# A channel mix by one 96x96 block for each time half, with 20 unread identity products ahead of its loop

## The reference

```python
att = jnp.einsum('bnd,bmd->bnm', left, xf) / jnp.sqrt(jnp.float32(dk))
att = jax.nn.softmax(att, axis=-1)
return (att @ xf).reshape(sh) if requires_value else att
...
xc = jnp.swapaxes(_attention(jnp.swapaxes(x, 1, 2), W1_c, W2_c, True), 1, 2)
xt = jnp.swapaxes(_attention(jnp.swapaxes(xc, 1, 3), W1_t, W2_t, True), 1, 3)
```

## Time and profile before

| | us |
|---|---|
| median of three runs | 1740.32 |
| the three runs | 1743.68, 1740.32, 1725.60 |
| the profiled execution | 1733.57 |
| its span, first to last instruction | 1731.7 |
| TensorE busy in the span | 1425.5 (82%), mean granted clock 0.90 |
| VectorE, ScalarE, GpSimd busy | 1051.8, 768.2, 609.1 |

### The profile page before, as it was taken

How to read it: one execution, slowest core, us unless ns; L and a number is a source line. 1 busy time by engine, 2 the same in 40 slices (tenths; PEclk the granted TensorE clock), 3 DMA queues, 4 the chain that set the end, 5 groups by cost and what they waited for, 6 DMA issues and landing times. The chain is left out here.

```text
span 1731.7 us, 27002 instructions
## 1 busy us (share of the span) xinstructions
PE 1425.5 (82%) x8422; PEld 1185.3 (68%) x8422; DVE 1051.8 (61%) x2259; ACT 768.2 (44%) x1222; POOL 609.1 (35%) x910
## 2 busy tenths in 40 slices
PE   6698999997582599999999956788999996377676
PEld 5596887886582488888888846687888885244443
DVE  5323788887348445444445326463788887488885
ACT  5322555554350233233333225223555554288885
POOL 1100456556212445566555321000455656100000
PEclk9799999999675699999999965798999999599999
DMA  7451121211581255565555278821121221112322
GB/s 237 123 157 38 47 73 64 78 58 64 192 265 57 69 115 112 131 140 99 112 124 109 31 161 288 261 83 37 47 82 55 81 68 60 55 56 84 100 88 64
DMA packets 97738, 180.13 MB, mean 104 GB/s; under 512 B 15184, under 2 KB 33152, under 8 KB 97668
## 3 DMA queue, kind: packets, MB, share of 16 engines
q1 hardware_dynamic: 75396, 135.16, 24.8%
q0 software_dynamic: 16384, 31.51, 10.6%
q10 hardware_dynamic: 5888, 12.59, 2.0%
HBM read 113.12 MB, written 66.10 MB: 103 GB/s over the span
## 5 line engine op out<-in xcount | busy, mean ns | idle before, releaser
L922 PE MATMUL g_y<-L_z,L_pt 128*128 128x192 f32 x1024 | 195.4, 334 | 1.5 <-ACT L_pt L1137 0.5
L922 PEld LDWEIGHTS g_y<-L_z,L_pt 128*128 128x128 f32 x1024 | 165.2, 192 | 6.8 <-ACT L_pt L1137 6.8
L1082 POOL TENSOR_TENSOR L_xr<-L_xr,L_lnb 128x192 f32<-128x192 f32 x128 | 105.5, 852 | 177.8 <-DMA L_xr<-x 92.0
L1455 POOL DMA_INDIRECT sums<-x_yo,x_places x64 | 102.9, 1609 | 141.9 <-ACT x_yo L1658 131.9
L1129 ACT ACTIVATE L_e<-g_s,L_nm 128x512 f32<-128x512 f32 x128 | 88.0, 687 | 78.8 <-DVE L_nm L970 77.5
L890 PE MATMUL g_z<-L_kw,L_xnT 96*128 96x192 f32 x512 | 91.8, 331 | 20.6 <-DVE L_v L1000 20.4
L1089 POOL TENSOR_TENSOR L_t<-L_rstd 128x48 f32<-128x48 f32 x96 | 28.9, 301 | 223.7 <-DVE L_rstd L1024 218.7
L1567 DVE TENSOR_TENSOR x_mid<-ex_g,x_sig 128x480 f32<-128x480 f32 (+1 forms) x48 | 31.4, 654 | 123.4 <-ACT x_sig L1649 123.4
L890 PEld LDWEIGHTS g_z<-L_kw,L_xnT 96*128 96x128 f32 x512 | 82.3, 189 | 29.9 <-DVE L_v L1000 29.9
L979 DVE SCALAR_TENSOR_TENSOR L_p<-L_e,L_rl,L_adj 128x512 f32<-128x512 f32 x128 | 99.1, 775 | 4.5
L970 DVE TENSOR_REDUCE L_nm<-g_s 128x1 f32<-128x512 f32 x128 | 87.5, 683 | 18.8 <-PE g_s L899 18.0
(11 more groups left out here) (345 smaller groups left out, 3890.6 us busy)
## 6 DMA issues: line engine op xcount, KB each, us to landing
L_xnT<-xn_rows SPq DMA_DIRECT2D x48, 384.0 KB, 3.3
x<-L_y SPq DMA_DIRECT2D x32, 384.0 KB, 2.6
xn_rows<-L_xnT SPq DMA_DIRECT2D x54, 192.0 KB, 3.9
L_xr<-in_x SPq DMA_DIRECT2D x24, 384.0 KB, 3.4
L_xr<-x SPq DMA_DIRECT2D x24, 384.0 KB, 3.4
L_raw<-xn_rows SPq DMA_DIRECT2D x16, 384.0 KB, 3.6
ff_xa<-x SPq DMA_DIRECT2D x16, 384.0 KB, 3.9
ff_xr<-x SPq DMA_DIRECT2D x16, 384.0 KB, 3.5
```

Source lines behind the costliest of these rows:

```text
L922: last = nc.tensor.matmul(out, pt[k % 2][:, P * c:P * c + P], z[q][:, c, :], start=False, stop=(c == NK - 1))
L1082: last = nc.gpsimd.tensor_tensor(v_, v_, gain(s.lnb), ALU.add)
L1455: nc.gpsimd.indirect_dma_start(sums, row(places[e % 2][:, 1, t:t + 1]), yo[t % 4][:, :], None, compute_op=ALU.add).then_inc(sent[t % 4], 16)
```

## The change

A time half's outputs depend on the same half's inputs alone. The changed kernel makes one 96 x 96 matrix for each item (16 channels x 6 time steps, the same for both halves) instead of two of 96 x 192. Each product then gives the 96 outputs of its own half and nothing is added up in PSUM; to keep the order of the outputs, channel by channel with 12 time steps each, a product writes 16 runs of 6 elements, 12 apart. The number of products is unchanged. Ahead of TensorE's loop stand 20 products of the 128 x 128 identity with itself into the first PSUM buffer, which the first item overwrites.

```diff
                 def big_matrix(b):
                     if b >= 2:
                         dve.wait_ge(mixed, ready(b - 2))
-                    for h in range(2):
-                        last = nc.vector.tensor_tensor(
-                            big[b % 2][0:HALF, h, :].rearrange("p (c t) -> p c t", t=T),
-                            s.rct[0:HALF, b * C:b * C + C].unsqueeze(2).to_broadcast([HALF, C, T]),
-                            s.tmask[:, h, 1, :].unsqueeze(1).to_broadcast([HALF, C, T]), ALU.mult)
-                    last.then_inc(big_done, 1)
+                    nc.vector.tensor_tensor(
+                        big[b % 2][0:HALF, 0, 0:HALF].rearrange("p (c t) -> p c t", t=TH),
+                        s.rct[0:HALF, b * C:b * C + C].unsqueeze(2).to_broadcast([HALF, C, TH]),
+                        s.tmask[:, 0, 1, 0:TH].unsqueeze(1).to_broadcast([HALF, C, TH]), ALU.mult).then_inc(big_done, 1)
...
                     for k in range(NK):
+                        cols = psm[z % 2][:, k // 2, CT * (k % 2):CT * (k % 2) + CT].rearrange("p (c t) -> p c t", t=T)
                         for h in range(2):
-                            last = nc.tensor.matmul(psm[z % 2][:, k // 2, CT * (k % 2):CT * (k % 2) + CT],
-                                                    xnT[z][0:HALF, h, P * k:P * k + P], big[z % 2][0:HALF, h, :],
-                                                    start=(h == 0), stop=(h == 1))
+                            last = nc.tensor.matmul(cols[:, :, TH * h:TH * h + TH],
+                                                    xnT[z][0:HALF, h, P * k:P * k + P], big[z % 2][0:HALF, 0, 0:HALF],
+                                                    start=True, stop=True)
                     last.then_inc(mixed, 1)
 
+                keep_awake(nc, s, psm[0][:, 0, 0:P], 20)
                 with pe.Fori(0, B // 8) as i:
```

## The result

The changed kernel took **1763.1 us** (median of 4 runs, 1760.15 to 1766.29) against 1735.24 for the kernel before (4 runs, 1725.6 to 1743.68): the ratio is 1.016, with a 95% interval of 1.010 to 1.023. Forecast were 1720 us and a range of 1708 to 1735. It is slower, and the forecast had it faster.

What follows compares the result with a forecast made beforehand. TensorE was taken to bound layer 0's mix and VectorE's rounding to end layer 1's. The terms -11.1 - 6.2 + 0.5 = -16.8 us, from 1737, gave 1720 us, range 1708 to 1735.

Steps and rivals of the forecast that it cites:

- What bounds the kernel: Channel mixes: TensorE bounds layer 0, busy 39.38 of 39.80 us at full clock; VectorE's weight rounding ends layer 1.
- The passes: Channel mix: a pass of 96 columns takes 0.111 us instead of 0.162, an item 1.78 us, 0.82 less.
- rival A: Mix passes faster, at 0.081 us, with loads then binding items: 1715 us; chance 0.12.
- B: Gapped PSUM writes keep a mix pass at 0.162 us, so no gain per pass: 1736 us; chance 0.15.
- The start and the identities: Start of both mixes: 20 identities delay layer 0's item 1 to 86.0 us, hidden by a later wait; no net cost.
- the wait before item 5: Both mixes: item 5 reuses the first slot and waits for its load, landing at 94.6 us in layer 0.
- The twelve items after it: Layer 0, items 5 to 16: 12 x 0.82 = 9.8 us saved, at 1.78 us an item.
- The size of the wait: TensorE's idle time before item 5: 1.7 us in layer 0, 2.3 in layer 1.
- Layer 1: Its mix ends with VectorE's rounding 6.2 us earlier, at 1153.9: 4.1 from items 5 to 9, 2.1 from shorter matrices.
- The projections behind the mix: Stage after layer 1's mix: between 1.4 us less and 4.0 more, taken as 0.5 us more.
- Rival C: Granted clock stays at 0.50 in both mixes, an item taking 3.5 us: slower, 1766 us; chance 0.06.
- the 24 identities: Profile row of 24 identity passes of 128 columns at full clock, 2.84 us: source of the 0.111 us pace.

Runs made afterwards that it cites:

- The filled wait: The changed kernel with 18 more unread identity products between items 4 and 5, where TensorE waits for a load: 1727.32 us, ratio 0.992 to the kernel before.
- the 128 columns: The changed kernel with each product streaming 128 columns, 32 of them unread zeros, into a gapless PSUM slot: 1725.34 us, ratio 0.988 to the kernel before.
- the late weights last: The changed kernel with the two 1 MB late weights issued after all 16 items' loads: 1726.57 us, ratio 0.989 to the kernel before.

## Why the prediction was wrong

- **What bounds the kernel**: right. TensorE's pace in layer 0, VectorE at the end of layer 1.
- **The passes**: right at full clock, 0.111 us forecast and measured. Neither rival A (0.081) nor B: writing runs of six with gaps costs nothing that is seen. The Trainium skill (Advanced Engine Details and Errata, "PSUM Cachelines") warns of non-contiguous accesses and asks for adjacent pairs. The runs agree with the second half and show no slowing by gaps: at full clock the first 32 passes took 3.55 us with runs of six and 3.54 without gaps.
- **The start and the identities: the step that failed.** The forecast found the wait before item 5, and then used it as a cover, "the identities cost nothing and bring nothing", at a clock that stayed up. It did not ask what TensorE's idleness in that wait does to the clock, nor whether the new stream could bring it back. The twelve items after it were costed at 2.4 GHz, 1.78 us, and took 3.41: this one term makes -9.8 us into +9.7 in layer 0, and in layer 1 -6.2 became +7.7. The filled wait shows that the idleness is the cause, the 128 columns that the stream's shape is what keeps the clock down.
- **The size of the wait** was off too: 4.2 us, not 1.7, and 3.6, not 2.3, in layer 1. That loads land in the order of issue does not fix how long each takes. In the changed kernel the load for item 5, though issued earlier, landed later in the stage than in the earlier trace rows:

```profile
L_adj<-in_L_conv_A SPq DMA_DIRECT2D x1, 1024.0 KB, 13.3
...
L_xnT<-xn_rows SPq DMA_DIRECT2D x1, 384.0 KB, 9.2
```

  These are the median us from issue to landing. The second late weight took 13.3 us instead of 11.3 and the load 9.2 instead of 5.9: 85.84 + 9.2 = 95.0, 17.3 us into the stage instead of 15.4. The three loads behind it were issued before it landed and ran beside it at the same total rate (283 GB/s from the stage's first load to that landing, 284 before), which I take for the reason; no run takes it apart. In the kernel with the identities alone the second late weight took 13.2 us too, with the items at their old pace, and the load for item 5 took 6.7, so faster items are not the whole of it.
- **Layer 1**: the end by VectorE was right wherever the clock stayed up (43.9 us with the late weights last; forecast for the change, 1153.9 + 0.3 - 1107.95 = 46.3). In the changed kernel 12 items of 3.41 us outlast VectorE's chain.
- **The projections behind the mix** were to cost 0.5 us more; they began at the low clock in both layers and the two stages cost 2.6 + 0.9 = 3.5, the 2.6 in layer 0, where the forecast had put nothing.
- **Rival C** had the price, 1766 against 1763, and the mechanism nearly: half clock from the first item, where in fact the first four ran at full clock and the wait brought the fall. At 0.06 it was far too low. The argument against it was the 24 identities that ran at full clock "at the same pace". They have the same pace and not the same load: 128 streamed columns to 128 of weights, against 96. The row that was asked for the pace was taken to answer for the clock.

  The Trainium skill (TensorE: Matmul & The Clock Gate, "HAM oscillation — how this bites in real kernels") tells of a kernel whose clock falls in each wait for a load, and of a cure, to reorder the loop so that matrix work goes on before the wait. The fall here, from 1.00 to 0.50 around a wait of 4.2 us, agrees, and so do the kernels with the wait taken away.

## What to carry to other kernels

When an edit makes TensorE's passes shorter, ask three things of the stage: what clock it starts with, whether the faster work now runs into a load that it used to trail, and whether the new stream brings the clock up again after a pause. A saving per pass that leaves the weights' load as the bound can be undone by the clock, and streaming a few columns more, which cost no time there, was the simplest repair here; moving loads that nobody waits for behind those that TensorE needs was the other. A row that shows a pace says nothing of the clock of another stream with the same pace.

## What was not expected of the hardware

Passes of 96 streamed columns with 128 columns of weights ran back to back for 54.8 us at 1.2 GHz without the clock rising, and the very same passes ran for 28.8 us at 2.4 GHz without its falling. With 128 columns it rose 4 to 5.5 us after the first pass (100.4 against 96.3, and 88.1 against 82.6). Short waits went either way: in layer 1 of the kernel with the late weights last the clock stayed at 1.00 until its last item although TensorE waited about 0.5 us for VectorE before each of the last three, and with the wait filled it fell after waits of the same size.
